# Half steps of a Mamba pipeline: items of head and tail placed anew on four engines, and a table set for exponential and logarithm named by hand

## The reference, cut to what matters

```python
xz = x @ in_w.T; xb, z = split(xz)          # 512 channels each
xb = silu(causal_conv4(xb) + cb)
dbc = xb @ xp_w.T                           # delta rank 16, B 16, C 16
delta = softplus(dbc_delta @ dtw.T + dtb)
dA = exp(delta[..., None] * -exp(a_log))    # 16 states
mi = delta[..., None] * B * xb[..., None]
v = 0.6 * v + mi;  h = dA * h + v;  y = sum_n(h * C)
y = (y + dp * xb) * silu(z);  out = x + y @ ow.T
```

## Time and profile before

| | us |
|---|---|
| median of three runs | 4443.42 |
| lowest, highest | 4441.43, 4452.27 |
| profiled execution, first to last instruction | 4448.6 |
| TensorE busy, share of the span | 3574.1, 80% |
| VectorE | 2793.3, 63% |
| GpSimd | 2081.9, 47% |
| ScalarE | 1980.3, 45% |
| TensorE's mean granted clock | 0.870 of full |

### The profile page before, as it was taken

The page is one execution under the profiler, slowest core; times in us unless marked ns, Lnnn a source line. Parts: engine busy times, 40 slices in busy tenths (PEclk is TensorE's granted clock), DMA queues, the critical chain, the costliest instruction groups (busy, mean ns, idle before and its releaser), DMA issues. The chain is left out here.

```text
span 4448.6 us, 88475 instructions
## 1 busy us (share of the span) xinstructions
PE 3574.1 (80%) x28540; PEld 2392.4 (54%) x28541; DVE 2793.3 (63%) x4863; ACT 1980.3 (45%) x4454; POOL 2081.9 (47%) x1206
## 2 busy tenths in 40 slices
PE   6888869936988889888875888888988884499980
PEld 4454546624555555555543555555555553388870
DVE  3444432345777777777755777777777776655545
ACT  1212112205656666566634666656666553233320
POOL 0101000014667666676652766667667675422216
PEclk8888878967999999999986999999999995599995
DMA  1000000011313222132221221312223224211113
GB/s 50 0 0 0 0 21 0 0 56 41 74 51 73 52 54 74 49 75 52 53 63 33 64 61 51 76 50 60 66 51 73 51 55 152 99 48 47 47 40 109
DMA packets 151619, 230.36 MB, mean 52 GB/s; under 512 B 25106, under 2 KB 83890, under 8 KB 149556
## 3 DMA queue, kind: packets, MB, share of 16 engines
q1 hardware_dynamic: 143156, 202.30, 17.1%
q0 software_dynamic: 8064, 23.08, 1.8%
HBM read 119.99 MB, written 23.59 MB: 32 GB/s over the span
## 5 line engine op out<-in xcount | busy, mean ns | idle before, releaser
L893 POOL TENSOR_TENSOR m_hc<-m_h,m_Cb 128x1024 f32<-128x1024 f32 x512 | 1204.9, 2354 | 766.3 <-DVE m_h L1014 446.9
L1014 DVE TENSOR_TENSOR_SCAN m_h<-m_dA,m_hlast,m_bank 128x256 f32<-128x256 f32 x2048 | 1354.3, 725 | 145.3 <-PE m_bank L1295 62.6
L1277 PE MATMUL m_bank<-m_hc,ident 128*128 128x512 f32 x2048 | 1210.2, 680 | 147.9 <-POOL m_hc L893 147.6
L1144 ACT ACTIVATE m_dA<-m_delta,m_rate 128x256 f32<-128x256 f32 x2048 | 894.1, 500 | 16.3 <-DVE m_h L1014 15.4
L1293 PEld LDWEIGHTS m_bank<-m_M,m_U 128*128 128x128 bf16 x8192 | 605.1, 101 | 362.4 <-DVE m_h L1014 223.8
L1293 PE MATMUL m_bank<-m_M,m_U 128*128 128x64 bf16 x8192 | 675.2, 197 | 128.5 <-DVE m_h L1014 118.8
L1295 PEld LDWEIGHTS m_bank<-m_M,m_U 112*128 112x128 bf16 x8192 | 578.5, 100 | 205.6 <-issue 173.3
L1295 PE MATMUL m_bank<-m_M,m_U 112*128 112x64 bf16 x8192 | 675.3, 197 | 0.0
L1277 PEld LDWEIGHTS m_bank<-m_hc,ident 128*128 128x128 f32 x2048 | 337.8, 205 | 197.0 <-POOL m_hc L893 164.5
L962 DVE SCALAR_TENSOR_TENSOR m_cv<-m_xpre,m_conv,m_cv 128x256 f32<-128x256 f32 x384 | 272.3, 750 | 22.7 <-ACT m_cv L1082 18.2
L1207 PE MATMUL m_bank<-m_pair,m_in 128*128 128x256 f32 x1024 | 267.7, 388 | 7.6 <-ACT m_cv L1082 3.8
(11 more groups left out here) (273 smaller groups left out, 5637.6 us busy)
## 6 DMA issues: line engine op xcount, KB each, us to landing
m_Cb<-m_c_rows SPq DMA_DIRECT2D x256, 256.0 KB, 3.2
m_M<-m_Mhi SPq DMA_DIRECT2D x128, 256.0 KB, 4.1
m_M<-m_Mlo SPq DMA_DIRECT2D x64, 256.0 KB, 3.9
m_U<-m_Uhi SPq DMA_DIRECT2D x128, 128.0 KB, 3.2
y_rows<-x_y SPq DMA_DIRECT2D x40, 256.0 KB, 2.1
m_U<-m_Ulo SPq DMA_DIRECT2D x64, 128.0 KB, 3.4
g_stage<-in_e_w SPq DMA_DIRECT2D x8, 1024.0 KB, 5.4
o_stage<-in_e_w SPq DMA_DIRECT2D x16, 512.0 KB, 4.7
```

Source lines behind the costliest of these rows:

```text
L893: nc.gpsimd.tensor_tensor(hc[:, n % 2], h[:, n % RING], Cb[:, g % 2, n % NG, :].unsqueeze(1).broadcast_to([P, KI, CM]), ALU.mult).then_inc ...
L1014: nc.vector.tensor_tensor_scan(h[:, n % RING, m, :], dA[:, n % RING, m, :], VB[(n % 2) * 2 + g][:, (m % 2) * CM:(m % 2 + 1) * CM], hlast[: ...
L1144: nc.scalar.activation(dA[:, n % RING, m, :], delta[:, par, m, :], ACT.Exp, scale=rate[:, m, n:n + 1]).then_inc(s["da_done"], 1)
L1277: last = nc.tensor.matmul(Y[half][:], net.ident[:], hc[:, n % 2, 2 * half:2 * half + 2, :], start=(n == 0), stop=(n == NS - 1))
```

## The change

OFF goes from 10 to 9, and items get new numbers. With OFF the half step of an item is its number minus 9 (or plus 23 for numbers below 9). The half steps before and after:

| item | engine | before | after |
|---|---|---|---|
| in-projection, eight pieces | TensorE | hs 28 to 31, 0 to 3 | hs 29 to 31, 0 to 4 |
| x-projection; B, C; delta | TensorE | 7; 9; 11 | 7; 8; 11 |
| u transposes; carry | TensorE | 20; 23 | 21; 23 |
| out-projection, two halves | TensorE | 7, 8 | 6, 9 |
| convolution, two groups | VectorE | 1, 3 | 1, 4 |
| clamp; series; delta | VectorE | 13; 16; 17 | 14; 18; 18 |
| Ulo; clo; residual | VectorE | 22; 25; 9 | 22; 27; 11 |
| x copy for the convolution, two groups | ScalarE | 30, 0 | 29, 0 |
| Silu of z; of xb | ScalarE | 5; 5 | 1; 4 |
| xp; Bs copies | ScalarE | 8; 10 | 6; 9 |
| far; Exp; square | ScalarE | 12; 13; 14 | 12; 12; 12 |
| Exp of delta; Ln | ScalarE | 15; 16 | 13; 14 |
| Ghi; Mhi, two halves | ScalarE | 12; 14, 17 | 11; 11, 19 |
| Uhi; chi | ScalarE | 21; 24 | 22; 22 |
| Gf; matrices | GpSimd | 11; 11, 13 | 10; 11, 11 |
| Mlo first; Glo; u; Mlo second | GpSimd | 15; 17; 18; 20 | 15; 17; 18; 20 |

(GpSimd's items of hs 2n and 2n + 1 both stand behind the product of state n - 1.) The load of the set `natural_log_exp_and_others`, which holds Exp and Ln, is issued by hand once at the start and behind each Silu of xb. The core of the diff:

```diff
-RING, LEAD, OFF, NG = 4, 2, 10, 2
+RING, LEAD, OFF, NG = 4, 2, 9, 2
...
-                    if at == 21:
+                    if at == 19:
                         pool.wait_ge(s["b_done"], 1 + q + 1)
                         nc.gpsimd.tensor_tensor(Gf[:], Bs[:].unsqueeze(2).broadcast_to([P, TM, NSUB, NS]),
...
+                    if at == 20:
                         matrix(q, 0)
-                    if at == 23:
+                    if at == 20:
                         matrix(q, 1)
...
-                    if at in (11, 13):
-                        g = (at - 11) // 2
+                    if at in (10, 13):
+                        g = (at - 10) // (13 - 10)
...
-                    if at == 26:
+                    if at == 27:
                         dve.wait_ge(s["square_done"], 1 + q + 1)
...
-                    if at == 9:
+                    if at == 11:
                         dve.wait_ge(s["out_psum"], 1 + t + 1)
...
-                    if at == 15:
+                    if at == 10:
                         act.wait_ge(s["gated_done"], 1 + q)
                         for g in range(2):
                             act.wait_ge(s["in_psum"], 1 + q * 4 + g + 3)
                             nc.scalar.activation(zs[:, par, 2 * g:2 * g + 2, :], halves((H0, H1)[g]), ACT.Silu
                                                  ).then_inc(s["z_done"], 1)
+                    if at == 13:
                         act.wait_ge(s["conv_done"], 1 + q * 2 + 2)
                         nc.scalar.activation(xb[:, par], cv[:], ACT.Silu).then_inc(s["xb_done"], 1)
+                        nc.scalar.preload_act_table_set("natural_log_exp_and_others")
...
-                    if at == 34:
+                    if at == 31:
                         act.wait_ge(s["carry_psum"], 1 + q + 1)
...
-                    if at in (7, 8):
-                        j = at - 7
+                    if at in (6, 9):
+                        j = (at - 6) // (9 - 6)
```

More of the change, by code:

```diff
@@ L853, in head @@
                         nc.gpsimd.tensor_tensor(rstd[:], mean[:], net.half[:, 0:TM], ALU.pow).then_inc(s["rms_out"], 1)
-                    if at == 6:
+                    if at == 4:
                         pool.wait_ge(s["conv_done"], 1 + q * 2)
@@ L863, in head @@
                                                 ).then_inc(s["gf_done"], 1)
+                    if at == 20:
                         matrix(q, 0)
-                    if at == 23:
+                    if at == 20:
                         matrix(q, 1)
-                    if at == 25:
+                    if at == 24:
                         matrix_low(q, 0)
-                    if at == 27:
+                    if at == 26:
                         pool.wait_ge(s["ghi_done"], 1 + q + 1)
@@ L988, in head @@
                                                     ).then_inc(s["ulo_done"], 1)
-                    if at == 35:
+                    if at == 36:
                         dve.wait_ge(s["chi_done"], 1 + q + 1)
@@ L1041, in _ @@
                 tail(NCM, 1, 3)
-                tail(NCM, 1, 9)
+                tail(NCM, 1, 11)
             @block.scalar
@@ L1064, in head @@
                                                  ).then_inc(s["rms_in"], 1)
-                    if at == 3:
+                    if at == 2:
                         act.wait_ge(s["rms_out"], 1 + q + 1)
@@ L1070, in head @@
                                                  ).then_inc(s["xr_done"], 1)
-                    if at == 5:
+                    if at == 4:
                         act.wait_ge(s["xT_psum"], 1 + q + 1)
@@ L1090, in head @@
                                                  ).then_inc(s["z_done"], 1)
+                    if at == 13:
                         act.wait_ge(s["conv_done"], 1 + q * 2 + 2)
                         nc.scalar.activation(xb[:, par], cv[:], ACT.Silu).then_inc(s["xb_done"], 1)
-                    if at == 18:
+                        nc.scalar.preload_act_table_set("natural_log_exp_and_others")
+                    if at == 15:
                         act.wait_ge(s["xp_psum"], 1 + q + 1)
@@ L1096, in head @@
                         nc.scalar.copy(xp, H0[0:RANK + 2 * NS, 0:CM]).then_inc(s["xp_done"], 1)
-                    if at == 20:
+                    if at == 18:
                         act.wait_ge(s["bc_psum"], 1 + q + 1)
@@ L1100, in head @@
                                        ).then_inc(s["b_done"], 1)
-                    if at == 22:
+                    if at == 21:
                         for g in range(2):
@@ L1105, in head @@
                                                  bias=-FAR, scale=-1.0).then_inc(s["far_done"], 1)
+                    if at == 20:
                         act.wait_ge(s["gf_done"], 1 + q + 1)
                         nc.scalar.copy(Ghi[:], Gf[:].rearrange("p j i n -> p j (i n)")).then_inc(s["ghi_done"], 1)
-                    if at == 23:
+                    if at == 21:
                         act.wait_ge(s["far_done"], 1 + q * 2 + 2)
                         nc.scalar.activation(cv[:], cv[:], ACT.Exp, bias=-FAR, scale=-1.0).then_inc(s["exp_done"], 1)
-                    if at == 24:
+                    if at == 21:
                         act.wait_ge(s["exp_done"], 1 + q + 1)
@@ L1114, in head @@
                                              ).then_inc(s["square_done"], 1)
-                    if at == 25:
+                    if at == 22:
                         act.wait_ge(s["clamp_done"], 1 + q * 2 + 2)
                         nc.scalar.activation(u[:], delta[:, par], ACT.Exp).then_inc(s["near_done"], 1)
-                    if at == 26:
+                    if at == 23:
                         act.wait_ge(s["near_done"], 1 + q + 1)
                         nc.scalar.activation(u[:], u[:], ACT.Ln, bias=1.0).then_inc(s["ln_done"], 1)
-                    if at in (24, 27):
-                        j = (at - 24) // 3
+                    if at in (20, 28):
+                        j = (at - 20) // (28 - 20)
                         act.wait_ge(s["mf_done"], 1 + q * TM + j + 1)
@@ L1211, in head @@
                             last.then_inc(s["in_psum"], 1)
-                    if at == 17:
+                    if at == 16:
                         pe.wait_ge(s["xb_done"], 1 + q + 1)
@@ L1218, in head @@
                         last.then_inc(s["xp_psum"], 1)
-                    if at == 19:
+                    if at == 17:
                         pe.wait_ge(s["xp_done"], 1 + q + 1)
@@ L1244, in head @@
                             last.then_inc(s["uT_psum"], 1)
-                    if at == 33:
+                    if at == 32:
                         pe.wait_ge(s["moved_next"], 1 + 3 * 16 * q)
@@ L1342, in _ @@
                     late(NCM, n, 1)
-                tail(NCM, 1, 7, False)
-                tail(NCM, 1, 8, False)
+                tail(NCM, 1, 6, False)
+                tail(NCM, 1, 9, False)
 def mamba_phases(net):
```

7 lines of the change are left out of this document (2 added, 5 removed).

## The result

The changed kernel takes 4272.43 us (median of four runs, 4259.96 to 4276.44) against 4445.69 for the kernel before: ratio 0.9606, 95% interval 0.9591 to 0.9622, 173 us saved. The profiled execution is 4274.6 us long.

A forecast was written before the change was run, and what follows sets the result against it. No engine is full; TensorE's standing still among in-order engines counts. One round 25.5 + 26.9 + 14.5 + 4.6 = 71.5, taken as 72.6 against 80.15; less low clock, 6.5 us saved over 30 chunks: 4248 us, range 4195 to 4300.

The forecast's parts named there:

- First part: TensorE, hs 0 to 9: the hs 6 waits go, a new xb wait comes, A of hs 9 ends at 25.5; gain 4.2 us.
- The wait for xb: TensorE ahead of the x-projection: a new wait of 2.2 us, xb wanted at 17.9 us and done at 20.0.
- the gain of 4.2: TensorE up to A of hs 9: 2.65, 1.28 and about 2 us of low clock go, 2.2 comes.
- Tables: ScalarE's table loads: four a chunk before and after, 1.28 us each, no drain; nothing saved in sum.
- the wait goes: GpSimd's 2.04 us stop, from VectorE waiting for ScalarE's logarithm before the scan of hs 18, disappears.
- Second part: GpSimd, from the product freed by A of hs 9 to the second Mlo's end: 26.9 us instead of 28.9.
- Third part: SP's queue after the second Mlo: hs 30 not before 66.9 us, a new TensorE wait of about 2.4.
- Low clock: TensorE behind the two new waits: nothing or 2 us each; 1.0 us a chunk taken in sum.
- hand-over and loop edge: Chunk's end: half of 1.44 us for the edge gives 72.2, hand-over times raise the chunk to 72.6.
- ScalarE as the bound: Four ScalarE items wait early, delaying VectorE's decays; slower from 29.3 us waiting a chunk, some 20 found; 4503 us, chance 0.09.
- VectorE's wait for the out-projection: Sign in the changed profile: VectorE's wait at L1003 under 3 us.

## Why the prediction came out right, point by point

**Total.** 4248 forecast, 4272 measured, within the range. 195 us forecast, 173 measured; 6.5 us a chunk against 5.7.

**First part (hs 0 to 9): right in place and size.** V of hs 6 without a wait; A of hs 9 was to end at 25.5, and the product that it frees starts at 1530.60 - 1504.59 = 26.0. The wait for xb was put at 2.2 and came out as 1.23 because V of hs 7 started at 17.3, not 16.4, after a wait of 0.56: the convolution took 5.93 us beside the gate and a product, where I took the old 4.80. xb itself was done at 20.1 against 20.0 forecast. The parts that I named for the gain of 4.2 (2.65, 1.28 and 2 less 2.2) add to 3.7; the 4.2 rests on the link by link sum alone.

**Tables: the count right, the worth wrong.** Four loads in place of four, no drain: the activation starts 0.01 us behind each load. By the Trainium skill ("ScalarE: Activation LUTs", What ACT_TABLE_LOAD costs) a switch would cost 1.38 us more; this trace does not agree (the decays end at 1522.30, the load starts at 1522.32 and takes 1.28, the Silu starts at 1523.61). The Trainium skill's rule to batch activations by set ("ScalarE: Activation LUTs", Table sets: the hidden batching unit) agrees in its direction: undoing the split gave 31 us. What I missed is that the two loads taken from around the logarithm were worth 55 us in the changed kernel and 71 in the kernel before. In the sum they stood only inside "the wait goes" (2.04 us of GpSimd), not as a term, and the second Mhi behind them in ScalarE's list, on which by the rows of that run most of the 55 hang, stood nowhere.

**Second part (GpSimd's run): right in kind, 0.8 us short.** 26.9 us forecast; from 1530.60 to 1558.26 it is 27.7. The wait of 2.04 went, and a wait of 0.70 for an accumulate of TensorE came in. The rest is an exchange between VectorE's long steps and GpSimd's. In the changed kernel (VectorE, then GpSimd):

```profile
1545.22 2.72 DVE L975 SCALAR_TENSOR_TENSOR m_pair<-m_pair,m_cv 128x1024 f32<-128x1024 f32 x1
1548.05 1.28 DVE L980 SCALAR_TENSOR_TENSOR m_u<-m_u,m_floor,m_pair 128x1024 f32<-128x1024 f32 x1
```

```profile
1544.48 2.37 POOL L894 TENSOR_TENSOR m_hc<-m_h,m_Cb 128x1024 f32<-128x1024 f32 x1
```

In the kernel before, again VectorE, then GpSimd:

```profile
1656.04 1.38 DVE L974 SCALAR_TENSOR_TENSOR m_pair<-m_pair,m_cv 128x1024 f32<-128x1024 f32 x1
```

```profile
1656.30 3.10 POOL L844 TENSOR_TENSOR m_Mlo<-m_Mf,m_Mhi 128x1024 bf16<-128x1024 f32 x1
```

Before, the series step started ahead of the first Mlo and the Mlo took 3.10 us; now it starts behind a product and takes 2.72 itself, the Mlo takes 2.15, and the product of 1548.18, which starts behind the next VectorE step (1548.05), takes 3.37 instead of 2.35. For GpSimd that is 0.95 less and 1.02 more, so the 0.8 is in the main the wait of 0.70. I had priced all of it by old durations; here they cancelled, which is luck, and in the convolution above they didn't.

**Third part (SP's queue): right.** From the end of Mlo to hs 30 I had 14.5 us; it is 1558.26 to 1572.93, 14.7. The wait was put at 2.4 and is 2.3 and 2.5 in these chunks. That it fits so closely is partly luck: TensorE was to be ready at 64.4 and was at 66.0 (its waits at hs 18 to 22 add to 3.05, not 1.7), and the queue was done at 68.3, not 66.9. The runs with four more transfers and with U first show that what is put into the queue or taken out of it ahead of clo comes out in the time.

**Low clock: right as a middle.** I allowed 1.0 us a chunk between 0 and 4. In the first chunk there is none: A of hs 30 takes 1.10 us. In the second the clock is 0.77 in the window from hs 30 on, where TensorE takes 7.42 us for what took 4.63 in the first (1572.93 to 1577.56), 1.02 of it the loop edge: 1.8 us. It does not come every second chunk, though. Of the 28 waits for clo inside the two layers (without each layer's last), 12 have hs 30 and 31 longer by 1.6 to 1.8 us, besides the loop edge; the others by 0.2 us at most. That is 0.7 us a chunk.

**Where 0.9 us a chunk was lost**: the start of the run 0.5 later (26.0 against 25.5), the run 0.8 longer, the queue 0.2, 1.5 in all. Against that, I had allowed 1.1 us a chunk for hand-over and loop edge, and the edge took half of 1.02, so 0.6 came back. **ScalarE as the bound** (the slower rival): it waits 72.97 - 48.30 = 24.7 us in a chunk, not the 20 I found, and holds VectorE 36 times between 1100 and 3500 us, 28.7 us in all and 1.3 at the longest (0.88 ahead of the scans of hs 9 here); in the kernel before it was 33.5 us. **VectorE's wait for the out-projection** fell to 1.3 us.

## What to carry to other kernels

In a pipeline of in-order engines, cut a round out of the dependencies and add it up link by link, the transfer queue included: the wait that is seen moves to the next link, and a single item moved past a stall may gain little until a filler moves with it. When an item is moved or shortened, ask what is listed behind it on its engine and which queue (here SP's) carries the delay on. Price a moved step by its new neighbours, not by its old duration.

## What the runs showed of the hardware that I had not expected

- Where a VectorE step of two inputs on 128x1024 f32 and a GpSimd step overlap, the one that started first takes its usual time and the other stretches. VectorE second: 2.72 us (1545.22, ends 1.09 after the product does) and 2.07 (1660.72 in the kernel before, ends 1.08 after). VectorE first: 1.28 to 1.38 us, and GpSimd's Mlo takes 3.10 instead of 2.15, a product 3.37 and 3.42 instead of 2.35.
- Six convolution steps take 3.69, 4.56, 4.80 and 5.93 us where a gate or product of GpSimd runs beside them for 1.2, 2.1, 2.4 and 3.8 us.
- Six transfers issued in ScalarE's list took 6.3 us there (5.9 in the next chunk), and its next activation stood 7.66 us; SP issued the same six in 4.5 us (5.7 in the next chunk, one of them 1.77).
- After a wait of 2.31 us for clo the clock stays at the upper level and after one of 2.51 it falls (0.77 in the window). The length of the wait does not decide: in the same trace hs 30 and 31 are longer by 1.6 us behind a wait of 1.93 and not behind one of 2.33. What decides is open.
